# Second attention of a hybrid block: the row maxima copied by ScalarE and subtracted by a second accumulating matmul, instead of being added to the query rows by VectorE

## The reference

```python
def _L0_attn_b_ref(x, Wqkv, bqkv, Wo, bo):
    B, N, D_MODEL, H = (4, 256, 128, 16)
    b, n, _ = x.shape
    qkv = x @ Wqkv.T + bqkv
    qkv = qkv.reshape(b, n, H, -1).transpose(0, 2, 1, 3)
    q, k, v = jnp.split(qkv, 3, axis=-1)
    scale = k.shape[-1] ** 0.5
    scores = jnp.einsum('bhqd,bhkd->bhqk', q, k) / scale
    attn = jax.nn.softmax(scores, axis=-1)
    out = jnp.einsum('bhqk,bhkd->bhqd', attn, v)
    out = out.transpose(0, 2, 1, 3).reshape(b, n, -1)
    return out @ Wo.T + bo
...
x = x + _L0_attn_b_ref(_layernorm(x, axis=-1), L0_attn_b_Wqkv, L0_attn_b_bqkv, L0_attn_b_Wo, L0_attn_b_bo)
```

## Time and profile before

| | us |
|---|---|
| three runs, median | 580.54 |
| three runs, lowest and highest | 578.9, 585.16 |
| profiled execution, its own time | 574.57 |
| profiled execution, span | 572.8 |
| mean granted clock of TensorE in it | 0.971 |

### The profile page before, as it was taken

The page is one execution under the profiler, slowest core; times in us unless marked ns, Lnnn a source line. Parts: engine busy times, 40 slices in busy tenths (PEclk is TensorE's granted clock), DMA queues, the critical chain, the costliest instruction groups (busy, mean ns, idle before and its releaser), DMA issues. The chain is left out here.

```text
span 572.8 us, 11532 instructions
## 1 busy us (share of the span) xinstructions
PE 517.6 (90%) x3757; PEld 390.4 (68%) x3757; DVE 432.7 (76%) x1105; ACT 344.8 (60%) x607; POOL 290.0 (51%) x276
## 2 busy tenths in 40 slices
PE   3878887899999999999788898988999999999996
PEld 3555564577888888888454555645678888888884
DVE  3678798569798898567677887989479796886663
ACT  3676746456555655666457767676865655555553
POOL 4765572146666756777421305020166656666664
PEclk9799988899999999999779999999999999999999
DMA  6358870213454344235641524310442444354340
GB/s 168 114 185 263 245 249 2 72 62 98 107 116 127 92 119 121 98 112 180 200 117 51 185 75 143 116 39 3 62 106 97 109 135 124 103 137 132 95 143 20
DMA packets 48549, 67.60 MB, mean 118 GB/s; under 512 B 6625, under 2 KB 18930, under 8 KB 48498
## 3 DMA queue, kind: packets, MB, share of 16 engines
q1 hardware_dynamic: 45392, 66.47, 39.9%
q10 hardware_dynamic: 3106, 0.48, 0.5%
HBM read 53.56 MB, written 13.37 MB: 117 GB/s over the span
## 5 line engine op out<-in xcount | busy, mean ns | idle before, releaser
L639 POOL TENSOR_TENSOR KS<-PT,QS 128x512 fp32r<-128x512 f32 x144 | 186.2, 1294 | 118.1 <-ACT QS L836 106.1
L831 ACT ACTIVATE bank<-bank 128x512 f32<-128x512 f32 x128 | 74.5, 582 | 98.5 <-PE bank L856 97.9
L1562 DVE TENSOR_TENSOR PT<-CS,bank 128x512 f32<-128x512 f32 x128 | 87.4, 683 | 45.1 <-PE bank L856 44.3
L854 PE MATMUL bank<-XH,WH 128*128 128x512 f32 (+1 forms) x288 | 115.4, 401 | 1.7 <-DVE PT L1434 1.5
L856 PE MATMUL bank<-XH,WL 128*128 128x512 f32 (+1 forms) x288 | 112.9, 392 | 0.0
L855 PE MATMUL bank<-XL,WH 128*128 128x512 f32 (+1 forms) x288 | 112.6, 391 | 0.0
L836 ACT ACTIVATE QS<-PT 128x512 fp32r<-128x512 f32 x144 | 90.1, 626 | 12.2 <-DVE PT L1567 11.8
L1458 DVE TENSOR_REDUCE MEXP<-bank 128x4 f32<-128x1024 f32 x64 | 78.2, 1223 | 22.8 <-PE bank L966 22.1
L1567 DVE TENSOR_TENSOR PT<-PT,bank 128x512 f32<-128x512 f32 x128 | 88.0, 687 | 9.5 <-ACT bank L831 1.6
L750 ACT ACTIVATE PT<-bank 128x1024 f32<-128x1024 f32 x64 | 65.6, 1025 | 40.1 <-PE bank L998 39.8
L1021 PE MATMUL bank<-PT,V 128*32 128x256 f32 (+1 forms) x1024 | 64.6, 372 | 0.3 <-ACT OTS L760 0.3
(11 more groups left out here) (185 smaller groups left out, 770.6 us busy)
## 6 DMA issues: line engine op xcount, KB each, us to landing
CS<-combine_rows SPq DMA_DIRECT2D x128, 256.0 KB, 3.2
head_rows<-HP SPq DMA_DIRECT2D x28, 256.0 KB, 3.0
QS<-head_rows SPq DMA_DIRECT2D x28, 256.0 KB, 2.7
KS<-head_rows SPq DMA_DIRECT2D x28, 256.0 KB, 3.0
head_rows<-PHI SPq DMA_DIRECT2D x14, 256.0 KB, 3.1
out_dram<-X SPq DMA_DIRECT2D x4, 256.0 KB, 3.7
stage<-in_L_ffn_gate_w_dram SPq DMA_DIRECT2D x5, 192.0 KB, 3.8
stage<-in_L_ffn_up_w_dram SPq DMA_DIRECT2D x5, 192.0 KB, 4.0
```

The source lines that it names most:

```text
L639: pool.tensor_tensor(GL[:, (u - 1) % 3, :], GG[:, (u - 1) % 3, :], GH[:, (u - 1) % 3, :].bitcast(f32), ALU.subtract).then_inc(F.gl, 1)
L831: act.activation(TH[:, u, :] if u < SHARED else G[u % 3][:, :], G[u % 3][:, :], ACT.Silu).then_inc(F.th, 1)
L854: pe.matmul(out, wh, vh, start=start, stop=False)
L1562: dve.tensor_tensor(ab, CS[:, e % CBUFS, :], U[u % 3][:, :], ALU.mult).then_inc(F.b, 1)
```

## The change

`queries_with_maxima` goes from VectorE. In its place ScalarE copies `MT` to `Q2` (`maxima_rows`), between its two exponentials of a slot and ahead of the biased rows. `Q2` no longer holds the queries, only the maxima and zeros, so `scores_less_maxima` makes each output by two matmuls into the same place of the bank: keys by queries, 24 rows deep, then keys by `Q2`, 25 rows deep, added to it. The two heads of the pair now take turns within each half t.

```diff
@@ ScalarE @@
+                def maxima_rows(i):
+
+                    if not 0 <= i < ITEMS:
+                        return
+                    act.wait_ge(A.mt, i + 1)
+                    if i >= 2:
+                        act.wait_ge(A.s2[0], 2 * i - 2)
+                    act.activation(Q2[:, i % 2, :], MT[:, 0:SEQ], ACT.Copy).then_inc(A.q2, 1)
+
...
                     probabilities(1, n - 4)
+                    maxima_rows(n - 3)
                     if g - 1 in PROJECTION_SLOT and c + 1 < CHUNKS:
                         biased_rows(c + 1, PROJECTION_SLOT[g - 1], PJ)
                     probabilities(0, n - 4)
@@ TensorE @@
-                    pe.wait_ge(A.q2, i + 1)
                     if i + 2 - x < ITEMS:
                         pe.wait_ge(A.mx[x], i + 3 - x)
                     else:
                         pe.wait_ge(A.ex[x], i)
-                    for h in (2 * x, 2 * x + 1):
-                        r = slice(32 * h, 32 * h + 3 * HD + 1)
-                        for t in range(2):
-                            o = SEQ * b + P * t
+                    pe.wait_ge(A.q2, i + 1)
+                    heads = (2 * x, 2 * x + 1)
+                    for t in range(2):
+                        o = SEQ * b + P * t
+                        for h in heads:
+                            r = slice(32 * h, 32 * h + 3 * HD)
+                            pe.matmul(S[h][:, SEQ * t:SEQ * (t + 1)], KS[r, j, o:o + P], QS[r, j, SEQ * b:SEQ * (b + 1)],
+                                      start=True, stop=False)
+                        for h in heads:
+                            r = slice(32 * h, 32 * h + 3 * HD + 1)
                             m = pe.matmul(S[h][:, SEQ * t:SEQ * (t + 1)], KS[r, j, o:o + P], Q2[r, i % 2, :],
-                                          start=True, stop=True)
-                        m.then_inc(A.s2[x], 1)
+                                          start=False, stop=True)
+                            if t:
+                                m.then_inc(A.s2[x], 1)
@@ VectorE @@
-                def queries_with_maxima(i):
...
-                    dve.tensor_tensor(Q2[:, i % 2, :], MT[:, 0:SEQ], QS[:, j, SEQ * b:SEQ * (b + 1)].bitcast(f32),
-                                      ALU.add).then_inc(A.q2, 1)
...
                     maxima(0, n - 2)
-                    queries_with_maxima(n - 3)
                     maxima(1, n - 2)
```

## The result

| | before | changed |
|---|---|---|
| median of four runs, us | 580.66 | 591.58 |
| lowest and highest, us | 578.9, 585.16 | 589.1, 592.11 |
| profiled execution, own time and span, us | 574.57, 572.8 | 591.98, 590.2 |
| mean granted clock in it | 0.971 | 0.952 |

The ratio of the changed kernel to the one before is 1.022, with a 95% interval from 1.019 to 1.026. Timed again beside other kernels it was 588.80 against 578.18, ratio 1.019 (1.011 to 1.027). The two pairs of medians are 10.9 and 10.6 us apart. The forecast was 601.0, range 589 to 610: slower was right, the size was forecast at almost twice what came.

The account below looks back on a forecast made before the run. The prediction took a ring of ScalarE and TensorE in the second attention as the bound. Its terms, 14.3 + 3.8 + 2.3 + 1.1 - 1.0 = 20.5 us, on the median 580.54 gave 601.0 us, range 589 to 610.

Parts of the forecast that it names:

- What bounds the kernel: Second attention, slots 4 to 35: ScalarE and TensorE wait for each other in turn, neither busy all the time.
- ring: Exponential, scores, second product, next exponential: 1.74 us for ScalarE and TensorE alone, VectorE adding 0.08; forecast to become 2.16.
- plain half: Time from one exponential's start to the next without side work, two in a slot; forecast to grow from 1.825 to 2.16.
- The matmuls added: Four more matmuls in each second product, two more steps, 0.42 us; 14.3 us over 42 waiting halves at full clock.
- the five at half clock: Five waiting halves of the second attention at the lower clock, each growing by 2 x 0.38, 3.8 us.
- 2.3, 1.1 and -1.0: Terms in us: copies ahead of biased rows in 6 halves; 11 exponentials that did not wait; VectorE's waits saved.
- one step only: Rival: each second product grows by 0.21, a plain half by 0.125, giving 590.0 us; chance 0.13.
- The foot of the range: Lower end of the forecast range, 589 us, set to take in the one-step case.
- The copy and the heads' order: ScalarE's copies take 0.38 each, hidden in plain halves, 2.3 us at biased rows; heads taking turns gives nothing.
- the relief: VectorE spared 32 additions, 13.2 us of work, in halves where it waits for scores anyway; counted as 1.0 us gained.
- ScalarE's waits: ScalarE's waits for the second product between 290 and 400 us, forecast to rise from 33.8 to about 50 us.
- The baseline: Added loss of 20.5 us put on the median of runs, 580.54, not on the quick profiled execution, 574.57.

Follow-up runs that it names:

- The matmuls alone: Changed kernel, but VectorE instead of ScalarE copies the maxima to Q2, products unchanged: 588.47 against 577.48 us for the kernel before, ratio 1.020.
- the copy alone: Changed kernel with the old four-matmul second product and ScalarE writing only zeros to Q2: 578.03 against 577.48 us before, ratio 1.0005.
- one arrangement: Changed kernel with the second product put ahead of the other pair's scores in TensorE's order: 602.22 against 578.18 us before, ratio 1.042.
- its two variants with the same products: Changed kernel with VectorE copying the maxima (588.47 us), and with the old program order of heads (587.25 us); each ratio 1.020 to before.

## Why the prediction was right, and where it was off

**What bounds the kernel: right.** That the changed kernel is slower, and by which path, was forecast; the size was not. ScalarE and TensorE wait for each other in a ring with one second product in every half. The matmuls alone gave the full loss (1.020), the copy alone none (1.0005), and the plain half equals its parts: 1.02 for the exponential, 0.05 to the scores, 0.11 to the product, 0.79 to the next exponential, 1.97, as 344.10 to 346.07 shows.

**The matmuls added: the mis-sized term.** "Two more steps of 0.20 to 0.22, that is 0.42" was 0.24. Of 24 or 25 rows the trace of before held only runs of two matmuls on one set of partitions, that is only first steps, and the first is the long one; the second and all later ones are 0.12, up to six deep. A plain half so grew by 0.175, not 0.34.

The trace of before did hold the warning, in runs of three matmuls on the whole array at full clock, as here in slot 18:

```profile
338.96 0.48 PE L854 MATMUL bank<-XH,QKH 128*128 128x512 f32 x1
...
339.28 0.39 PE L855 MATMUL bank<-XL,QKH 128*128 128x512 f32 x1
...
339.51 0.40 PE L856 MATMUL bank<-XH,QKL 128*128 128x512 f32 x1
```

The first step there is 0.32 and the second 0.23, shorter by 0.09; in the product it is 0.20 and 0.12, shorter by 0.08. The rows of the weight loads show where the first step's excess lies. Those of the second product at 332.70 in the kernel before, and then those of the one at 345.28 in the changed kernel:

```profile
332.67 0.21 PEld L998 LDWEIGHTS bank<-Q,KS 25*128 25x128 f32 x2
...
332.78 0.22 PEld L998 LDWEIGHTS bank<-Q,KS 25*128 25x128 f32 x2
```

```profile
345.25 0.18 PEld L1009 LDWEIGHTS bank<-QS,KS 24*128 24x128 f32 x1
...
345.36 0.22 PEld L1013 LDWEIGHTS bank<-Q,KS 25*128 25x128 f32 x2
...
345.48 0.22 PEld L1009 LDWEIGHTS bank<-QS,KS 24*128 24x128 f32 x2
...
345.61 0.22 PEld L1013 LDWEIGHTS bank<-Q,KS 25*128 25x128 f32 x2
```

The loads follow each other after 0.11 to 0.13 from the start. The first matmul starts 0.03 after its load does (345.28 against 345.25), each later one 0.11 to 0.12 after (345.48, 345.60 and 345.72 against 345.36, 345.48 and 345.61). So the gap between the first two matmuls is longer than the pace of the run, and the pace of 0.11 could be read before the change, from 332.67 and 332.78. What sets that pace no run here separates.

With 0.24 in the sum's own steps: 42 x (1.74 + 0.24 - 1.825 = 0.155) = 6.5; for the five at half clock some 0.35 each (the third exponential followed the second after 2.45 and not 2.13; the others that lie whole at that clock in both traces grew by 0.33 to 0.39), 1.8; 2.3, 1.1 and -1.0 as they stood. That is 10.7, against 10.6 and 10.9 between the medians. So close a match is partly luck, since the 2.3 of the copy came out at some 1.0, and 63 halves at the growth counted at full clock make 8 to 9 us. The rival "one step only", 590.0, came out closest in time, but by neither of its mechanisms: the products run in as many steps as forecast, of a shorter kind. The foot of the range came from that rival. That it took in the measured time is luck as well: two short steps of 0.12 come to nearly the same as its one of 0.21.

**The copy and the heads' order: right, but for the biased rows.** The copy took 0.38, with idle time behind it in plain halves. Ahead of the biased rows it was to cost 6 x 0.38 = 2.3 us. In the copy alone it cost 0.26 in four such halves and nothing in the fifth, some 1.0 us. In slot 19 it runs straight into the biased rows (354.99 to 355.25) and the half stays at 2.33, as it was (342.45 to 344.78). The heads side by side in either order was right too.

**VectorE: right.** It left the ring, and its waits for scores rose from 17.2 to 39.1, by more than the 13 us it was spared. With the old product the relief was worth 0.03 for a plain half (7.17 against 7.30 for four); with the longer one it made no difference where the copy ran (7.99 and 8.00).

**ScalarE's waits: wrong.** They were to rise from 33.8 to about 50 us and stayed at 32.8. Three things were left out: a copy in every second gap takes 0.38 from the wait without taking time, some 24 x 0.38 = 9 us in that stretch; the product grew by little more than half of the forecast; and the fixed window now holds 47 exponentials and not 55. Over the whole stage these waits rose from 39.8 to 44.4 us. A wait that is shortened by hidden work is not a gain, and one that stays the same doesn't mean that nothing got longer.

**The baseline.** Putting the sum on the median of the runs was right: the profiled execution of before lay 6 us under its median, and the difference of medians is 10.6 to 10.9, not 17.4.

## What to carry to other kernels

When work of an engine that waits is traded for matmuls, ask which ring the matmuls stand in: here the engine relieved was waiting anyway, and the one loaded stood in every round. Before costing a longer run of an instruction by the gap between two of them, look for a run of three or more, if need be of another shape, and at the weight loads: the first gap may be the dear one. And an order that takes an instruction from behind one wait may put the next instruction behind another: name both before swapping.

## What was not expected of the hardware

- Matmuls on one set of partitions (24 or 25 rows, 256 columns, f32r) follow each other after 0.20, then every 0.12, in runs of four and of six; two sets do so side by side, whatever their order in the program.
- In one arrangement, scores that had ended at 342.84 released VectorE only 0.37 us later, 0.15 after matmuls ahead of them in the program ended. Ends in program order would explain it, and the Trainium skill says so ("TensorE: Matmul & The Clock Gate", Part 3); the next maxima at 345.39 come 0.16 after the product's last matmuls again. With products of two steps the rows couldn't tell. It stays open.
- The mean clock over a launch was 0.954 to 0.977 with products of two steps (33 launches of the kernel before), 0.952 to 0.977 with four (the changed kernel and its two variants with the same products), but 0.923 to 0.930 with six. The order counts too: with the product put first it was 0.937 to 0.949 with four steps and 0.948 to 0.963 with two. Filling the idle time moved it by under 0.01. Why six steps bring the lower level so much more is open.
